# Moving weight copies, norm transposes, decay arguments and output-weight loads in a norm / block-sparse linear / gated FFN / state-space mixer kernel

## The reference

```python
x = L0_attn_a_data                                   # (2, 512, 512) float32
x = x + attn_a(layernorm(x), mask, weight, bias)     # linear, 32x32 blocks switched off by the mask
x = x + ffn(layernorm(x), gate, up, down)            # 512 -> 1792 -> 512, int weights
x = x + attn_b(layernorm(x), ...)                    # state-space mixer, 128 heads of 64
x = x + ffn(layernorm(x), gate, up, down)            # the same weights again

def ffn(x):
    w = (imatrix - zeros) * scales                   # one row of zeros and scales per 128 inputs
    return (silu(x @ gate_w) * (x @ up_w)) @ down_w

def attn_b(x):
    gate, hBC, dt = split(x @ in_proj_w.T)           # 8192, 8192 + 2*8*128, 128 columns
    x, B, C = split(silu(causal_conv(hBC, 4 taps) + conv_b))
    dt = softplus(dt + dt_bias)
    # in chunks of 128 tokens, per head h (A = -exp(A_log)):
    M = (C B^T) * exp(segment_sum(A*dt))             # "arguments", exp, masked product
    y = M (x*dt) + (C * exp(cumsum)) state + D*x     # "outputs"; state carried from chunk to chunk
    y = y * rsqrt(mean(y*y)) * norm_w * silu(gate)
    return y @ out_proj_w.T
```

## Time and profile before

| | us |
|---|---|
| three runs, median (lowest, highest) | 2160.19 (2159.47, 2160.98) |
| profiled execution: device time / span | 2159.47 / 2157.7 |
| TensorE busy (13386 matmuls) | 2110.9 |
| VectorE busy | 1693.8 |
| ScalarE busy | 1393.3 |
| GpSimd busy | 881.9 |
| mean granted TensorE clock | 0.993 |

### The profile page before, as it was taken

The page is one execution under the profiler, slowest core; times in us unless marked ns, Lnnn a source line. Parts: engine busy times, 40 slices in busy tenths (PEclk is TensorE's granted clock), DMA queues, the critical chain, the costliest instruction groups (busy, mean ns, idle before and its releaser), DMA issues.

```text
span 2157.7 us, 37467 instructions
## 1 busy us (share of the span) xinstructions
PE 2110.9 (98%) x13386; PEld 1736.3 (80%) x13386; DVE 1693.8 (78%) x2682; ACT 1393.3 (65%) x1901; POOL 881.9 (41%) x622
## 2 busy tenths in 40 slices
PE   7999988999999999999999999999999999999999
PEld 6788867788888888888888888888888888877887
DVE  7555467989898888888898889898887988875554
ACT  5322247878787778777787877787777778742221
POOL 1222124445454544454454544544544545422221
PEclk9999989999999999999999999999999999999999
DMA  5544214333333333233323333333333233354441
GB/s 200 164 144 141 68 65 129 113 99 97 109 99 98 109 99 117 95 104 108 99 99 108 103 95 116 104 121 95 99 105 107 92 111 98 112 184 155 138 146 39
DMA packets 128644, 241.89 MB, mean 112 GB/s; under 512 B 14048, under 2 KB 48608, under 8 KB 128224
## 3 DMA queue, kind: packets, MB, share of 16 engines
q1 hardware_dynamic: 128480, 239.73, 35.1%
HBM read 234.17 MB, written 5.51 MB: 111 GB/s over the span
## 4 chain that ended last, share of the span: by engine, by line
PE 80%; DVE 2%; issue 2%; ACT 1%; DMA 1%; POOL 0%; SPq 0%; DVEq 0%; ACTq 0%; POOLq 0%
PE ring L958 35%; PE ring L1058 15%; PE bank_e L406 6%; PE yt L1039 6%; PE st L1023 4%; PE yt L1045 4%; PE bank_e L417 3%; PE xt L1010 3%; PE arg L996 2%; PE xt L971 1%; DMA w_raw<-w_in 0%; PE arg L1088 0%; DVE xc L1379 0%; PE st L983 0%; DVE m_xn L1490 0%
## 5 line engine op out<-in xcount | busy, mean ns | idle before, releaser
L958 PE MATMUL ring<-m_lnt,w_sb 128*128 128x512 f32 x3456 | 860.6, 399 | 1.9 <-DVE xc L1379 1.9
L958 PEld LDWEIGHTS ring<-m_lnt,w_sb 128*128 128x128 f32 x3456 | 632.4, 189 | 129.6 <-DVE xc L1379 2.1
L1643 POOL TENSOR_TENSOR w_sb<-w_raw,w_sb 128x512 fp32r<-128x512 f32 x288 | 401.8, 1400 | 174.1 <-ACT w_sb L1202 173.9
L1658 POOL TENSOR_TENSOR ysq<-ysq,y 128x512 f32<-128x512 f32 x126 | 163.0, 1294 | 654.0 <-ACT y L1246 654.0
L1058 PE MATMUL ring<-wo,ygs 128*128 128x512 f32 x1536 | 369.6, 390 | 2.0 <-issue 2.0
L1058 PEld LDWEIGHTS ring<-wo,ygs 128*128 128x128 f32 x1536 | 287.2, 188 | 63.3 <-issue 2.7
L1379 DVE SCALAR_TENSOR_TENSOR xc<-ring,cw,xc 128x511 f32<-128x511 f32 (+2 forms) x384 | 286.2, 745 | 21.7 <-ACT xc L1214 12.6
L1214 ACT ACTIVATE xc<-ring,cb,cw 128x512 f32<-128x512 f32 x128 | 99.1, 775 | 218.1 <-PE ring L958 218.1
L1648 POOL TENSOR_TENSOR wo<-wo_raw,wo 128x512 fp32r<-128x512 f32 x128 | 214.0, 1672 | 0.0
L1202 ACT ACTIVATE w_sb<-w_raw 128x512 fp32r<-128x512 f32 x288 | 177.1, 620 | 27.5 <-DMA w_raw<-w_in 27.4
L1039 PE MATMUL yt<-em,x_dt 128*64 128x128 f32 x2048 | 183.9, 279 | 3.4 <-DVE state L1421 3.4
(11 more groups left out here) (199 smaller groups left out, 3167.0 us busy)
## 6 DMA issues: line engine op xcount, KB each, us to landing
w_raw<-w_in SPq DMA_DIRECT2D x288, 256.0 KB, 4.3
ce<-e_t SPq DMA_DIRECT2D x128, 384.0 KB, 4.2
wo_raw<-w_out SPq DMA_DIRECT2D x128, 256.0 KB, 4.4
f_gu_q<-gu_w SPq DMA_DIRECT2D x28, 512.0 KB, 3.8
f_gu_zr<-gu_z SPq DMA_DIRECT2D x28, 512.0 KB, 4.5
f_gu_sr<-gu_s SPq DMA_DIRECT2D x28, 512.0 KB, 5.4
f_dn_q<-dn_w SPq DMA_DIRECT2D x28, 256.0 KB, 3.5
f_dn_zr<-dn_z SPq DMA_DIRECT2D x28, 256.0 KB, 4.2
```

The costliest lines, as they stand in the source:

```text
L958: mm = nc.tensor.matmul(dst[:], w_sb[:, u % WR, wp, k * P:(k + 1) * P], lnt[:, xp, k, b * S:(b + 1) * S], start=(i == 0), stop=(i == 3 * K ...
L1643: nc.gpsimd.tensor_tensor(w_sb[:, u % WR, 1], w_raw[:, u % NR], w_sb[:, u % WR, 0].bitcast(F32), ALU.subtract).then_inc(w_lo, 1)
L1658: nc.gpsimd.tensor_tensor(part, part, y[:, k % 2], ALU.add).then_inc(ysq_done, 1)
```

## The change

Work is neither added nor removed: every engine issues the instructions that it issued before. Their places differ.

1. In the first pair of both FFNs, VectorE and ScalarE do the next pair's first weight tile (`deq_gu(1, 0)`, `high_gu(1, 0)`) ahead of `hidden(0, 1, 0)`, as the other pairs do.
2. The transposes of tiles 6 and 7 move from within the up matmuls of unit 0 (after 8 of 12) to behind the whole unit. In `f1` those of tiles 4 and 5 move from ahead of the gate matmuls of unit 0 to behind them.
3. `high_gu(0, 1)` stands ahead of `norm_high` of tiles 6 and 7; in `f2`, tiles 4 and 5 come ahead of the centering of 6 and 7 on ScalarE, and VectorE does `deq_gu(0, 1)` between tiles 5 and 6.
4. In `f2` the first weight tile's `scale_gu(0, 0)` moves from step 129 to step 128 on VectorE (ahead of the last `gate`), and `high_gu(0, 0)` on ScalarE ahead of `y_high(127)`.
5. The output weight tile 126 is loaded and split one step later.
6. In the mixer's steps 1 to 127 `outputs(k-1)` comes ahead of `arguments(k)`.

```diff
@@ ffn, VectorE, first pair (the same on ScalarE with high_gu)
                         if not first:
                             hidden(p, 0, 0)
                             hidden(p, 0, 1)
-                        else:
-                            hidden(p, 1, 0)
                         if not last:
                             deq_gu(p + 1, 0)
-                        if not first:
-                            hidden(p, 1, 0)
+                        hidden(p, 1, 0)
                         hidden(p, 1, 1)
@@ ffn, TensorE
                                 u = 2 * j + half
+                                if first and u == 1:
+                                    lead.tensor_between(pe, n)
...
                                     if first and u == 0 and part == 1:
-                                        lead.tensor_up(pe, n)
+                                        lead.tensor_middle(pe, n)
                                     for i, (k, (a, b)) in enumerate((k, ab) for k in range(KT) for ab in PASSES):
-                                        if first and u == 0 and part == 1 and i == 2 * KT:
-                                            lead.tensor_in_up(pe, n)
@@ Mixing, ScalarE
                 center(n, 3)
+                high_gu(0, 1)
                 high(n, 3)
-                high_gu(0, 1)
@@ Mixing, TensorE
+                pe.wait_ge(self.res, T - 3)
+
+            def tensor_middle(self, pe, n):
                 norm_turn(pe, n, 4)
                 norm_turn(pe, n, 5)
-                pe.wait_ge(self.res, T - 3)
-
-            def tensor_up(self, pe, n):
                 pe.wait_ge(self.res, T - 1)
 
-            def tensor_in_up(self, pe, n):
+            def tensor_between(self, pe, n):
                 norm_turn(pe, n, 6)
                 norm_turn(pe, n, 7)
@@ output weights
-            return [k - 2] if 2 <= k < K - 1 else [K - 3, K - 2] if k == K - 1 else [K - 1] if k == K else []
+            return [k - 2] if 2 <= k < K else [K - 2, K - 1] if k == K else []
...
-                for k in range(K):
+                for k in range(K + 1):
...
-                    if 1 <= k < K:
-                        load_out(k - 1 if k < K - 1 else K - 1)
-                    if k == K - 2:
-                        load_out(K - 2)
+                    if k >= 1:
+                        load_out(k - 1)
@@ Mixer, TensorE
-                    if k < K:
-                        arguments(k)
                     if 1 <= k <= K:
                         outputs(k - 1)
                     if k < K:
+                        arguments(k)
                         turn_x(k)
@@ Mixer, ScalarE, step K
                         norm_center_act(act, n, 0)
                         norm_center_act(act, n, 1)
+                        high_gu(0, 0)
...
                         norm_high(act, n, 0)
                         norm_high(act, n, 1)
-                        high_gu(0, 0)
@@ Mixer, ScalarE, end
                 norm_root(act, n, 3)
+                norm_high(act, n, 4)
+                norm_high(act, n, 5)
                 norm_center_act(act, n, 6)
                 norm_center_act(act, n, 7)
-                for t in range(4, T):
-                    norm_high(act, n, t)
                 high_gu(0, 1)
+                norm_high(act, n, 6)
+                norm_high(act, n, 7)
@@ Mixer, VectorE
-                    if k == K + 1:
-                        scale_gu(0, 0)
                     for i, t in out_tiles(k - 1):
                         accumulate(i, t)
+                    if k == K:
+                        scale_gu(0, 0)
...
                 norm_shift(dve, n, 3)
-                sub_gu(0, 1)
-                for t in range(4, T):
-                    norm_low(dve, n, t)
-                scale_gu(0, 1)
+                norm_low(dve, n, 4)
+                norm_low(dve, n, 5)
+                deq_gu(0, 1)
+                norm_low(dve, n, 6)
+                norm_low(dve, n, 7)
```

More of the change, by code:

```diff
@@ L370, in body @@
                             hidden(p, 0, 1, first)
-                        else:
-                            hidden(p, 1, 0, first)
                         if not last:
                             high_gu(p + 1, 0)
-                        if not first:
-                            hidden(p, 1, 0, first)
+                        hidden(p, 1, 0, first)
                         hidden(p, 1, 1, first)
```

## The result

The changed kernel takes 2173.64 us (median of 6 runs, 2171.16 to 2174.30), the kernel before 2159.83 us (6 runs, 2158.59 to 2160.98): ratio 1.0062, 95% interval 1.0049 to 1.0076. It is 13.8 us slower; I had forecast 2166 us, a little under half of that, in a range that ended at 2171. The profiled execution took 2174.03 us, its span is 2172.3 us, 14.6 us above the span before.

What follows compares the result with a forecast made beforehand. TensorE, busy 98% of the span, was taken as the bound. Terms 3.1 - 2.8 - 4.1 + 1.3 + 3.4 = +0.9, plus clock charges +4.6, +1.7, -0.8, gave +6.4: 2166 us, range 2159.5 to 2171.

Steps and rivals of the forecast that it cites:

- Lead of f1: First FFN, before unit 1: later transposes and copies start unit 1 3.1 us later, with 3.4 us idle in one piece.
- First pair: Both FFNs: new 1.9 us wait before down phase, old mid-phase idle and its 1.2 GHz stretch gone: -2.8 and -4.1 us.
- the +6.4: Whole kernel: the forecast's summed slowdown in us, charges for falls of the clock included.
- The clock: TensorE behind new idles: falls to 1.2 GHz at 1.7 us each, charged +4.6 for three long idles, +1.7 for two shorter.
- Steps 1 to 127: Mixer, outputs ahead of arguments: steady steps covered; +1.0 us in steps 1 to 4, 0.3 at step 95; together +1.3.
- the early fall: Mixer: 1.2 GHz behind the early 2.06 us idle may not come again, that idle now being 1.8: -0.8 us.
- Into f2: Before the second FFN: step 129's projection behind 3.5 us idle instead of 2.04; 1.3 us left after savings, bounds +0.2 to +2.0.
- slow: Rival, mixer steps: the new order of array shapes costs 0.04 us a step, 5 us over 127, 2171 us; 8%.
- fast: Rival, mixer steps 1 to 127: one shape change falls away, 0.1 us a step, -12.7 us, giving 2154 us; 4%.
- the clock did not hold: Denies the rival that most new TensorE idles cost no clock: +0.9 to +3 us, 2161 to 2163.5 us; 25%.
- the leads were not cheap: Denies the rival that both FFNs' reordered copies hide and idles stay under 2 us: -3 us, 2157 us; 8%.

Runs made afterwards that it cites:

- the changed kernel with matmuls: The changed kernel plus 12 unused matmuls of 512 columns in the idle ahead of unit 1 of both FFNs: 2168.16 us, ratio 1.0036.
- edits 2 and 3 with matmuls: Kernel before plus edits 2 and 3, and 12 unused matmuls in the idle ahead of unit 1 of both FFNs: 2162.93 us, ratio 1.0021.
- the other order in the first pair: Kernel before, first pairs: next tile's subtraction ahead of the third hidden, scaling behind it, second weight tile behind four residual adds: 2150.71 us, ratio 0.9959.
- edit 1 with GpSimd held back: Kernel before plus edit 1; in first pairs GpSimd's second down-weight low part waits until VectorE scaled the next weight tile: 2157.75 us, ratio 0.9991.

## Why the prediction was wrong

The direction and each place were right: slower, through waits of 3 to 4 us at unit 1 in both FFNs and at step 129, a new wait at the head of the first down phases, steady mixer steps unchanged. The size was wrong, and most of it is one term.

- **Lead of f1, forecast +3.1.** From where the gate matmuls or transposes start (48.05 before, 49.31 after) unit 1 came 8.05 us later before and 10.99 after: +2.9. Right, with a wait of 3.17 us for 3.4. The 1.3 us by which that start itself slid comes from ahead of all edits; the profiled kernels whose work there is that of before slid by 0.7 to 1.6 us as well. Edits 2 and 3 alone, +9.2, stand beside the 5.2 of my terms and two falls of the clock at 1.7, 8.6 in all.
- **First pair, forecast -2.8 and -4.1: the step that failed.** It said that the third `hidden` would be 1.9 us late, and that the old idle time and "the 1.7 at 1.2 GHz behind it" would go. The wait was 2.98 and 2.99 us. I had taken the scaling at 1.23 us, as it was when GpSimd was quiet; at its new place GpSimd makes the low part of a down weight, and it took 2.20. The low part behind it took 1.00 for 0.69, in a second collision that I did not have either. Held apart at the scaling, the wait was 2.18 in f1. (The durations that I listed also add up to 74.6 rather than 74.45 with the smallest handovers.) With a wait as long as the old one, a fall of the clock came too, in both FFNs: 48 down matmuls took 12.62 and 14.05 us, and 11.04 where nothing waited. From unit 1 to the second pair the traces give +1.45 us (f1: 32.16 before, 33.61 after) and +1.56 us (f2: 33.52 and 35.08), both with the fall at unit 1 in them. Forecast, with the charges for the clock, were -0.4 and -1.7. That is 5.1 of the 8.2 us by which the trace exceeds the +6.4: 2.2 are the longer waits, 2.9 the falls behind them, for which I had charged 1.7 and which cost 1.6 and 3.0. By the medians, edit 1 alone measured +1.0 us where my terms with half a fall each give -5.2; of these 6.2 us the traces put only part in the pairs, so their nearness to the 7.4 that the forecast lacks is in part luck.
- **The clock.** I charged 6.3 us for falls at new places and took 4.4 as gone with the old ones. Five waits in the changed kernel all had a fall, two of them of 6.8 us; there were 10.2 us more of 1.2 GHz in all than before (27.2 and 17.0, the long norm ahead of the mixer left out). At half speed that is at most 5.1 us, an estimate, since part of the stretches is idle. A stretch does not cost as much as the idle time ahead of it, as I wrote, but 1.7 us beside 2.94 and 2.7 beside 3.33. Placing matmuls in two of these waits took away 5.9 us, of which 3.1 can be placed there.
- **Steps 1 to 127, forecast +1.3, less 0.8 for the early fall.** The trace has +1.27 from the first step to the last projection of step 128, edit 6 alone has +1.0 us between the medians (the interval reaches from -0.6 to +3.2). Steady steps: 0.02 us in 54. The 1.3 is right; other profiled kernels with the steps of before were up to 3.5 us longer there too, so the firm part is what all four kernels with the edit share, about 1.1 us. The -0.8 is not borne out: the early stretch of 1.2 GHz did not come, and nothing like the 1.7 us that I put on it was gained. Where it was missing without edit 6, with matmuls in the leads, steps 1 to 127 were 0.1 us shorter.
- **Into f2, forecast +1.3.** The projection of step 129 started 1.8 us later against `outputs(127)`, as I had it (8.93 - 7.13). Its idle was 3.84 for 3.5. The clock then stayed low for 6.8 us, so none of the 1.8 was won back. The scaling took 1.70 us beside GpSimd, inside my bounds (the upper one, two whole GpSimd operations of 1.29 and then 1.23, comes to +2.8 by its own terms and not +2.0). What I did not have is `y_low(126)` ahead of it, 1.80 us for 0.82 beside the low part of an output weight. Where it took 0.68 to 0.82 (the changed kernel with matmuls; edits 4 and 5), the idle was 2.96 and 3.10 us; where it took 1.80 again (the changed kernel without edits 2 and 3), 3.84. So the nearness of 3.84 to my 3.5 is in part luck. The Trainium skill's rule of the shared port (SBUF — State Buffer, "Who interferes with whom") is borne out by both collisions of a scaling, 1.70 and 2.20 us where it takes 1.23 alone. I applied it to this scaling and not to the one in the first pair, where it would have given the longer wait, though not the fall behind it.
- **The rivals.** The steps were neither slow nor fast; the clock did not hold; the leads were not cheap. None of them had the collision in the first pair.

## What to carry to other kernels

When work moves in one engine's queue, take its duration at the new place: list what the engine that shares a port with it does there, for every moved instruction and not only for the one at which the trace happens to show it. An idle time of TensorE that is merely moved, at the same length, kept its price here, the stretch of 1.2 GHz behind it included; count that stretch as gone only if the idle is gone. The fix for a down phase that waits for residual adds was to put the first four adds ahead of weight work that is due later, with a subtraction moved into a gap of VectorE, which was worth 9.0 us together.

## What the runs showed of the hardware

- Ahead of the fifth down tile of the first FFN, TensorE waited 2.93 to 2.95 us in eight profiled kernels. 1.2 GHz followed in five (the kernel before, the one with edits 2 and 3, and those with edit 2, 3 or 4 alone) and not in three (edit 6; edits 4 and 5; edits 2 and 3 with matmuls), where the 24 matmuls behind it took 5.72 or 5.73 us, not 7.2 to 8.5. The same wait at the same place can go either way.
- Of nine idles of 2.04 us ahead of step 129's projection, four were followed by 1.2 GHz (edit 1; edits 2 and 3; edit 2; the other order in the first pair). Longer ones there, of 2.86 to 3.84 us, were followed by it in five kernels of five. Waits of 2.18 and 2.57 us ahead of the down phases (edit 1 with GpSimd held back) were not, nor one of 3.11 us ahead of unit 1 (edit 3).
- VectorE's 1.23 us product of two SBUF tiles took 2.20 us with 1.1 us of a GpSimd operation beside it; the GpSimd operation took 1.54 for 1.29. Which of the two engines pays can differ with the starts alike to some hundredths of a microsecond: `y_low(126)` took 1.80 us when GpSimd's operations had begun 0.02 us ahead of it (they took 2.96), and 0.68 us in the kernel where they had begun 0.01 ahead (they took 4.04). What decides it, no run shows.
- Outputs then arguments then transposes costs TensorE the same as arguments, outputs, transposes, to under 0.001 us a step.
